# A two-layer decoder on one NeuronCore: the stretch from the routed experts to the third attention put into one table of steps per engine

## What is computed

```
x = x + L0_ffn(layernorm(x))                       # 8 experts of 256, top 2 per token, plus a shared expert
x = x + L1_attn(layernorm(x))                      # per batch and head, 24 of the 128 queries
x = x + L1_xattn(ctx, ctx, layernorm(x), mask)     # all queries against the context

# L1_attn, cut:
q, k, v = proj(Wq, bq), proj(Wk, bk), proj(Wv, bv)
q_norm = jnp.sum(jnp.abs(q), axis=-1)
_, index = jax.lax.top_k(q_norm, u)                # u = 24
scores = where(causal, q @ k.T * scale, -inf)
sel_attn = softmax(take_along_axis(scores, index))
attn_output[index] = sel_attn @ v                  # the other rows stay 0
out = attn_output @ Wo + bo
```

## Time and profile before

| | |
|---|---|
| median of 3 runs | 722.93 us (719.76 to 728.8) |
| the profiled execution | 720.38 us |
| its span, first to last instruction | 718.7 us |
| mean granted clock of TensorE | 0.903 |
| PE busy / DVE / ACT / POOL in the span | 79% / 60% / 40% / 34% |

### The profile page before, as it was taken

One profiled execution on the slowest core, in us unless ns is written; L12 is line 12 of the kernel. 1 busy time (PEld: TensorE's weight loads), 2 busy tenths in 40 slices (PEclk: granted clock), 3 DMA queues, 4 the chain that ended last, 5 costly groups with the idle time before them and its releaser, 6 DMA issues.

```text
span 718.7 us, 14894 instructions
## 1 busy us (share of the span) xinstructions
PE 569.8 (79%) x4679; PEld 413.6 (58%) x4679; DVE 434.5 (60%) x1157; ACT 290.9 (40%) x679; POOL 243.0 (34%) x364
## 2 busy tenths in 40 slices
PE   3689996889987979898727898876989984574992
PEld 1344444566764659897515686643666652454991
DVE  4879887666766575456373465554556624677443
ACT  2675422245555215454203466530435542302660
POOL 6745503301011666253640113224000002372652
PEclk9899999999999979999868899995999988577997
DMA  9974988653500166532301000363445300013114
GB/s 282 326 126 132 277 237 230 162 132 82 135 8 5 42 244 215 170 86 67 79 26 36 0 2 1 100 155 83 126 99 122 70 2 2 0 46 102 34 35 136
DMA packets 87494, 75.72 MB, mean 105 GB/s; under 512 B 10457, under 2 KB 80753, under 8 KB 84513
## 3 DMA queue, kind: packets, MB, share of 16 engines
q1 hardware_dynamic: 82544, 66.80, 34.5%
q0 software_dynamic: 3296, 6.79, 3.2%
q10 hardware_dynamic: 1584, 1.26, 0.6%
HBM read 41.59 MB, written 32.98 MB: 104 GB/s over the span
## 4 chain that ended last, share of the span: by engine, by line
PE 48%; DVE 20%; DMA 9%; issue 8%; POOL 6%; ACT 4%; SPq 3%; DVEq 1%; POOLq 0%; ACTq 0%
PE ps L2330 5%; PE ps L1864 5%; PE ps L2197 3%; PE ps L2162 3%; PE ps L2432 3%; PE ps L2444 3%; PE ps L2342 2%; PE ps L2181 2%; POOL xs_scr L839 2%; PE ps L2158 2%; DMA f<-k_scr 2%; SPq L433 2%; PE ps L2015 2%; PE ps L1860 2%; PE ps L2176 2%
## 5 line engine op out<-in xcount | busy, mean ns | idle before, releaser
L1445 DVE TENSOR_REDUCE negm<-ps 128x4 f32<-128x512 f32 x128 | 84.3, 688 | 57.1 <-PE ps L2162 53.9
L1026 ACT ACTIVATE wa<-ps 128x1024 f32<-128x1024 f32 x64 | 65.5, 1024 | 70.6 <-PE ps L2181 64.5
L2330 PE MATMUL ps<-nT,f 128*128 128x128 f32 x368 | 52.0, 288 | 2.6 <-DVE wb L1657 1.2
L2330 PEld LDWEIGHTS ps<-nT,f 128*128 128x128 f32 x368 | 47.9, 204 | 3.6 <-DVE wb L1657 1.6
L2197 PE MATMUL ps<-wa,f 128*32 128x128 f32 x1024 | 40.2, 284 | 4.0 <-ACT wa L1026 1.5
L1936 PE MATMUL ps<-identb 128*128 128x512 bf16 x100 | 34.2, 401 | 7.8 <-DVE negm L1445 3.9
L710 POOL DMA_INDIRECT x_scr<-y_tok,selT x32 | 31.9, 996 | 23.8 <-ACT stack L1134 10.7
L844 POOL DMA_INDIRECT y_scr<-f,stack x23 | 25.6, 1114 | 30.3 <-DVE f L1803 24.8
L2162 PE MATMUL ps<-stack 75*128 75x128 bf16 x352 | 35.6, 225 | 0.0
L2162 PEld LDWEIGHTS ps<-stack 75*128 75x128 bf16 x352 | 28.4, 101 | 12.2 <-issue 2.4
L1529 DVE COPY f<-w_gu 128x512 f32 x46 | 20.4, 442 | 22.0 <-issue 10.5
(11 more groups left out here) (399 smaller groups left out, 1464.8 us busy)
## 6 DMA issues: line engine op xcount, KB each, us to landing
k_scr<-parts SPq DMA_DIRECT2D x48, 192.0 KB, 3.0
q_scr<-parts SPq DMA_DIRECT2D x48, 192.0 KB, 2.8
stack<-k_scr SPq DMA_DIRECT2D x11, 600.0 KB, 7.2
stack<-q_scr SPq DMA_DIRECT2D x11, 600.0 KB, 5.5
w_w<-in_w SPq DMA_DIRECT2D x2, 2048.0 KB
wb<-q_scr SPq DMA_DIRECT2D x5, 600.0 KB
f<-k_scr SPq DMA_DIRECT2D x5, 600.0 KB
x_scr<-sel SPq DMA_DIRECT2D x2, 1472.0 KB, 10.2
```

The source lines that it names most:

```text
L1026: link.release(act.activation(wa[:, u % 2, :], BF[u % 2], ACT.Exp, scale=SCALE), hWA.filled, hWA.at(stage, n * 4 + u), hB.freed)
L1445: v.tensor_reduce(negm[:, g4 * 4:g4 * 4 + 4, j], A[u % 2].rearrange("p (h k) -> p h k", h=4), AX.X, ALU.max, negate=True).then_inc(hA.free ...
L2330: last = mm(A[x % 2][:, c * S:(c + 1) * S], gu_of[x % NGU][:, c * S:(c + 1) * S], nT[:, k % 2, q * S:(q + 1) * S], start=True, stop=True)
```

## The change

The steps of the five named parts, from tile 21 on, get names of their own, and one table `LATE` per engine gives their order up to the end of the third attention: `tg`, `tk`, `td` are a tile's gate and up product, the turning of a group and the down product, `tc` and `tp` VectorE's weight copy and product, `ts`, `to`, `tn` ScalarE's share; `ga` are the two gathers of one batch; `comb` and `stat` the combine and statistics of a block; `normx` its normalisation, now on ScalarE with scale and bias (GpSimd's `mrstd` makes the two numbers); `turnx`, `projq`, `projk`, `projv`, `tokq`, `heads`, `pick`, `turns`, `seld` the projected pair; `pk`, `pf`, `qp`, `oq`, `pt`, `sc`, `lo`, `ex`, `tu`, `ec`, `sv`, `rc`, `ob`, `pu`, `pl`, `at` the sixteen picked rows; `outp`, `back`, `res`, `stat2`, `rstd2`, `norm2`, `turn2`, `projq2`, `split2` a late block; `A`, `B`, `V`, `M`, `X`, `o`, `x`, `P`, `E`, `N`, `e`, `K`, `s`, `c` the attention's steps as in `WOVEN`. The loop over tiles ends at tile 22; loops in the attention and the order `STEP` go. The first pair's picked rows 0 to 7 come before the second pair's heads; the first eight scores of the attention stand among rows 14 and 15. The 28 warming matmuls go. The first pair's steps rotate over three banks, the second pair's and the late blocks 0 to 2 share `Z`, block 3 uses `T`.

Places in SBUF change with it: keys and queries of the projected pairs move from the gate and up weights to the stack (`room`, over the tiles' rows), the rows' buffers from the stack to the gate and up weights, the picks and the new queries to the down weights, row sums get a tensor of their own; waits for the old users are added. SyncE loads step 0's keys after the second pair's heads, and keys of steps 1 and 2 before the second store; step 3's stack is loaded between the two last stores.

```diff
-        k1 = [flat_gu[:, i * 2 * BT:(i + 1) * 2 * BT] for i in range(2)]
-        q1 = [flat_gu[:, (2 + i) * 2 * BT:(3 + i) * 2 * BT] for i in range(2)]
+        k1, q1 = ([room[:, (2 * i + k) * 2 * BT:(2 * i + k + 1) * 2 * BT] for i in range(2)] for k in range(2))
         spent = w["down"][:, :, :, :].rearrange("p e c d -> p (e c d)")
-        new_q, rest_q = [spent[:, s * BT:(s + 1) * BT] for s in range(2)], spent[:, 2 * BT:3 * BT]
-        pick32, q_bd, e_row, e_col, o_bd, put = ([room[:, (2 * k + s) * HU:(2 * k + s + 1) * HU] for s in range(2)]
+        pick32, q_bd, e_row, e_col, o_bd, put = ([flat_gu[:, (2 * k + s) * HU:(2 * k + s + 1) * HU] for s in range(2)]
                                                  for k in range(6))
-        pick16 = [room[:, 12 * HU + s * HU // 2:12 * HU + (s + 1) * HU // 2].bitcast(bf16) for s in range(4)]
+        pick16 = [spent[:, s * HU // 2:(s + 1) * HU // 2].bitcast(bf16) for s in range(4)]
+        new_q, rest_q = [spent[:, 2 * HU + s * BT:2 * HU + (s + 1) * BT] for s in range(2)], spent[:, 2 * HU + 2 * BT:]
+        norm_T = [oT[:, 0, :], oT[:, 1, :], nT[:, 0, :], nT[:, 1, :]]
...
+        small = sb("row_sums", [128, 6 * NC])
...
+        three = (U, Bk[0][:, 0, :], Bk[1][:, 0, :])
+        first_turns, later_turns = ([s for s in LATE["PE"] if s[:-2] in READ_LATE and place(s) == n] for n in range(2))
+
+        def late_bank(step):
+
+            return (lambda: three[first_turns.index(step) % 3], lambda: Z, lambda: T)[place(step)]()
...
+                sp.wait_ge(gu_done, N0)
+                sp.wait_ge(pe_front, after("heads.1"))
                 load_k(a, 0, slot(0))
-                sp.wait_ge(qk1_ready, 3)
-                load_k(a, 2, slot(2))
                 store_pair("qp2", 0, queries, [], range(1))
                 sp.wait_ge(hP[0].freed, hP[0].free("qp2", 1))
+                sp.wait_ge(down_done, N0)
                 load_q(a, 0, slot(0))
+                sp.wait_ge(dve_front, after("comb.3"))
+                sp.wait_ge(slots_stored[1], 16 * PER)
+                load_k(a, 1, slot(1))
+                load_k(a, 2, slot(2))
                 store_pair("qp2", 0, queries, [], range(1, 2))
                 sp.wait_ge(hP[1].freed, hP[1].free("qp2", 1))
-                sp.wait_ge(attnT_done, 2 * B)
+                sp.wait_ge(scored, HB)
+                sp.wait_ge(q_picked, HB)
                 load_q(a, 1, slot(1))
-                load_k(a, 1, slot(1))
+                store_m(a, 0, slot(0))
+                sp.wait_ge(scored, B)
+                sp.wait_ge(q_picked, B)
                 load_q(a, 2, slot(2))
-                store_m(a, 0, slot(0))
+                store_m(a, 1, slot(1))
                 store_pair("qp2", 1, queries, [], range(1))
-                store_m(a, 1, slot(1))
+                load_stack(a, 3, slot(3))
+                store_m(a, 2, slot(2))
...
+            def gathers(b):
+
+                h = b // HB
+                g.wait_ge(slots_stored[h], 16 * PER)
+                if h == 0:
+                    g.wait_ge(slot_out, NT0 + b + 1)
+                for k, dst in enumerate((y_tok, second)):
+                    g.indirect_dma_start(dst[:, b, :], None, x0_scr[h],
+                                         bass.IndirectOffsetOnAxis(ap=pos0_i[:, k * B + b:k * B + b + 1], axis=0))\
+                     .then_inc(rows_back[b // GB], 16)
+
+            def pick_copy(b):
+
+                g.wait_ge(gu_ready, N0)
+                g.wait_ge(pick16_ready, b + 1)
+                if b > 1:
+                    g.wait_ge(q_picked, b - 1)
+                g.tensor_copy(pick32[b % 2], pick16[b % 4]).then_inc(pick32_ready, 1)
...
+                if kind == "normx":
+                    act.wait_ge(pool_front, after("mrstd.%d" % n))
+                    if n < 2:
+                        act.wait_ge(dve_front, after("te.1"))
+                    else:
+                        act.wait_ge(pe_front, after("turnx.%d" % (n - 2)))
+                    for j in range(GB):
+                        tok = n * GB + j
+                        last = act.activation(xn_tm[:, p, j, :], x_tok[:, tok, :], ACT.Identity, scale=rstd[:, tok:tok + 1],
+                                              bias=from_mean[:, tok:tok + 1])
...
+                elif kind == "absq":
+                    act.wait_ge(pe_front, after("projq.%d" % n))
+                    act.wait_ge(pe_front, after("su.3", "ro.3") if n < 2 else after("heads.0"))
+                    last = act.activation(f[:, p, :], late_bank("projq.%d" % n), ACT.Abs, bias=col["bq1"])
...
+                alone = dict(ec=e_columns, pu=scaled_places, ex=row_exps, at=placed_rows, ts=expert_silu, to=expert_out,
+                             tn=group_nT)
+                for s in WOVEN["ACT"] if a == 0 else LATE["ACT"]:
...
+                if kind == "comb":
+                    v.wait_ge(rows_back[n], 16 * GB * TOPK)
+                    for k, src in enumerate((y_tok, second)):
+                        for b in range(n * GB, (n + 1) * GB):
+                            last = v.scalar_tensor_tensor(out=x_tok[:, b, :], in0=src[:, b, :], scalar=wts[:, k, b:b + 1],
+                                                          in1=x_tok[:, b, :], op0=ALU.mult, op1=ALU.add)
+                        link(last, settle=True)
+                    v.sem_inc(dve_front, 1)
...
+            def row_maxima(b):
+                v.wait_ge(scored, b + 1)
+                if b > 1:
+                    v.wait_ge(e_row_ready, b - 1)
+                v.tensor_reduce(low1[b % 2], A[b % 2][:, 0:HU].rearrange("p (c k) -> p c k", c=NC), AX.X, ALU.max,
+                                negate=True).then_inc(low1_ready, 1)
...
+                    turns, depth = (first_turns, 3) if where == 0 else (later_turns, 1)
+                    turn_no = turns.index(this)
+                    if turn_no >= depth:
+                        read = reader(turns[turn_no - depth])
+                        pe.wait_ge(dict(ACT=act_front, DVE=dve_front)[PLACE[read][0]], after(read))
+                    elif where == 0:
+                        pe.wait_ge(dve_front, after("cc.1", "hd.3"))
+                        pe.wait_ge(act_front, after("sl.3"))
+                    else:
+                        pe.wait_ge(slot_out, N0 - 1)
...
-                keep_warm(T, 14)
...
+            def row_scores(b):
+                pe.wait_ge(pick16_ready, b + 1)
+                if b > 1:
+                    pe.wait_ge(e_row_ready, b - 1)
+                else:
+                    pe.wait_ge(prod_done, N0 - 1 + b)
+                pe.wait_ge(q_bd_ready, b + 1)
+                pe.wait_ge(act_front, after("evk.%d" % (b // GB)))
+                for c in range(NC):
+                    mm(A[b % 2][:, c * S:(c + 1) * S], pick16[b % 4][:, c * S:(c + 1) * S], causal[:, :], start=True,
+                       stop=False, skip_group_check=True)
+                    last = mm(A[b % 2][:, c * S:(c + 1) * S], q_bd[b % 2][:, c * S:(c + 1) * S],
+                              k1[b // HB][:, b % HB * S:(b % HB + 1) * S], start=False, stop=True, skip_group_check=True)
+                last.then_inc(scored, 1)
...
+                    if a == 2 and n == 0 and u < 2:
+                        pe.wait_ge(e_row_ready, B - 1 + u)
...
-            for x in range(N0 + 2):
-                if x < N0:
...
+            for x in range(NT0):
+                gate_up(x)
+                k, q = group_of(x)
+                if q == 0:
+                    slots_in(k + 1)
                 if x >= 2:
...
+                    expert_down(x - 2)
...
+    "PE": """
...
+            tg.45 td.44 turnx.1 projq.0 td.45 projk.0 projq.1 projv.0 tokq.0 heads.0 projk.1 projv.1 tokq.1 turns.0
+            pt.0 qp.0 pt.1 sc.0 qp.1 sc.1 tu.0 sv.0 tu.1 pl.0 sv.1 qp.2 pl.1 pt.2 sc.2 qp.3 pt.3 turnx.2 projq.2
+            sc.3 tu.2 qp.4 tokq.2 sv.2 qp.5 tu.3 qp.6 sv.3 turnx.3 pl.2 pl.3 projq.3 pt.4 pt.5 sc.4 sc.5 heads.1
+            qp.7 outp.0 tu.4 back.0 tu.5 sv.4 tokq.3 pl.4 sv.5 pt.6 sc.6 pl.5 turns.1 projk.2 pt.7 sc.7 tu.6 projv.2
+            sv.6 qp.8 turn2.0 pl.6 qp.9 tu.7 pt.8 sc.8 sv.7 qp.10 projq2.0 pl.7 tu.8 qp.11 outp.1 pt.9 sc.9 sv.8
+            projk.3 pl.8 qp.12 tu.9 pt.10 sc.10 back.1 sv.9 qp.13 pl.9 tu.10 projv.3 pt.11 sc.11 sv.10 pl.10 tu.11
+            pt.12 sc.12 turn2.1 sv.11 qp.14 projq2.1 pl.11 tu.12 pt.13 sc.13 outp.2 sv.12 qp.15 tu.13 back.2 sv.13
+            pl.12 pl.13 pt.14 sc.14 pt.15 sc.15 tu.14 A0.0 turn2.2 A1.0 tu.15 A2.0 A3.0 sv.14 A4.0 projq2.2 sv.15
+            pl.14 A5.0 A6.0 pl.15 A7.0 outp.3 A0.1 A1.1 M0.0 A2.1 back.3 A3.1 A4.1 A5.1 A6.1 B0.0 A7.1 B1.0 B2.0
+            A0.2 V0.0 A1.2 M0.1 B3.0 V1.0 A2.2 V2.0 X0.0 V3.0 A3.2 B0.1 o0.0 B1.1 A4.2 A5.2 turn2.3 A6.2 A7.2
+            projq2.3 V0.1 V1.1 M0.2 B2.1 X1.0 B3.1 o1.0 X0.1 V2.1 V3.1 o0.1 A0.3 A1.3 X1.1 A2.3 o1.1 B0.2 A3.3 A4.3
```

(25 more changed lines are left out.)

994 lines of the change are left out of this document (438 added, 556 removed).

## The result

The changed kernel takes 680.94 us in the median of four runs (679.15 to 683.63), against 721.95 for the kernel before beside it: a ratio of 0.942, 95% interval 0.935 to 0.949. That is 5.8% faster. The forecast was 670, its range 648 to 696. The profiled execution has a span of 679.9 us instead of 718.7.

The account below looks back on a forecast made before the run. Weak stages were taken as latency-bound, engines waiting in fixed order for chains of short operations. Stages 298.5, 46.1, 26.8, 78.4, 8.0, 86.0 and 123.2 gave a span of 667.0; forecast 670 us, range 648 to 696.

Parts of the forecast that it names:

- Parts 1 and 2: Tiles 23 to 45 take 3.0 us more, 46.1; then gathers and first picks, with row 2 starting at 371.4 us.
- Part 3: Rows 2 to 15 with second pair, three late blocks and VectorE's lumps: 78.4 us, rows ending at 449.8 instead of 477.5.
- VectorE's two lumps: Block 3's combine and statistics (4.8 us) and second top-24 chain (4.4), ahead of row work: 7.0 us together.
- it leaves little room: From 344 us on, VectorE's load is 76 of 113 us: not the bound, but with little room.
- Part 4: Start of the third attention: 8 us from rows' end to first transposed score, at 457.8 instead of 500.8.
- Part 5: The third attention's eight steps take 86 us instead of 94.7, ending at 543.8.
- Two DMA waits on the chain go: In the eight steps, the f load (7.55 us) and the last maxima's store (3.18) leave the chain: 10.7 us.
- A tighter weave: Rival, chance 0.16: TensorE never waits in the rows, which take 60.6 us instead of 78.4; whole time 653.
- One bank in a chain: Rival, chance 0.09: second pair and three late blocks share one bank, 24 turns, 19.2 us of waits; whole time 679.
- Loads late: Rival, chance 0.05: step 1's queries and step 3's stack queue behind stores; 10 us at the start and 7.55 stay: 689.
- One row in flight: Rival, chance 0.06: picked rows run one by one at about 8.7 us each instead of 3.55; whole time 743, slower.
- under 4.5 us a row with all else beside them: Sign of being right: from row 2 on, rows pass at under 4.5 us each, all other work included.

Follow-up runs that it names:

- the kernel with three banks: The changed kernel with all second-pair steps ahead of the first row, rotating over three banks, keys and values ahead of the picks' turn: 709.35 us, ratio 0.977.

## Why the prediction was right, and which of its steps failed

**The mechanism** held. The chain that the earlier trace rows named was latency with nothing beside it, and putting rows beside gathers and pair took it away: the stretch gave 43.9 us of the 46.0 predicted, 26.1 of them by that step, going by the kernel with three banks. The second pair ahead of the rows loses all of the kernel's gain, and with three banks most of what was lost is still missing.

**Parts 1 and 2, tiles and gathers,** were right to 0.6 us: 46.1 us as predicted, and 26.2 instead of 26.8 from there to row 2, with ten gathers, then row 2. Warming matmuls left out were costed at nothing; putting them back gained nothing.

**Part 3, the rows:** 82.3 us instead of 78.4, from two errors of opposite sign, so that it is as near as this is luck in part. I had counted 67.2 us of TensorE (49.7 + 9.7 + 7.8) and 11.2 of waits (4.2 for late blocks, 7.0 for VectorE's two lumps). TensorE had 76.65 to do and stood 5.6. The lumps were oversized: the waits for VectorE in the list above are 2.5 us (1.4, 0.7 and 0.4), 7.8 us more on VectorE made the rows 0.9 longer, and "it leaves little room" was wrong. The first scores, beside the last rows, had no price at all in the sum, though they are TensorE's work: without them it is busy 2.9 us less in the rows (73.72 in that kernel's window of 80.64). Products of rows 0 and 1 that slip behind row 2's copy are another 1.7 (93 placing and 90 summing matmuls are 15.5 and 15 rows of six, not 14, at 0.67). The other 4.8 of the 9.4 us I can't lay to one cause.

**Part 4, the start:** 6.8 us instead of 8.0. Load and split of the queries were hidden as said: TensorE stood 0.43 us for them.

**Part 5, the steps,** is the step that failed: 91.9 us instead of 86.0. "Two DMA waits on the chain go", 7.55 + 3.18 us, took a transfer's length in the chain for TensorE's loss. The earlier trace rows had it beside: TensorE was busy 86.16 of 94.7 us there, so all its waits together were 8.5, less than the 10.7 that I let go. The real idle time at the f load was 1.61; the new order in the kernel before gave 1.3 us, and those of busy time, while the idle time stayed 8.3. In the changed kernel the order is needed against a new lateness, worth 13 us.

**Outside the change** I took 298.5 us for granted; the front became 4.1 us longer. From 120 to 145 us the granted clock was 0.80 instead of 0.93, and from 190 to 232 it was 0.96 instead of 1.00, in code that no edit touched. What in the new program moves the clock there wasn't found.

**The rivals.** A tighter weave, 60.6 us from there to the rows' end, lay under TensorE's own 76.65. It took the 0.47 us off each row; but those are a wait of the weight loads, and over four rows of the kernel before TensorE's matmuls were busy all the time, so the pitch of 3.55 was their work already:

```profile
408.29:422.50 14.21, 14.21 (x119) 12.21 (x118) 9.50 (x20) 10.36 (x45) 2.03 (x4) 1.00 0.01 2
```

One bank in a chain gave 679, next to the 680.94 measured, but by another cause: its waits in the rows were 3.1 us and not 19.2. It is real only where the chain stands alone. Loads late did not come true as the kernel is made, and did when the load's place was undone. One row in flight: 14 rows took 5.9 us each with all that lies beside them, where my own sum had 5.6 (78.4/14). The 7.2 at which the gain would have gone counts a row alone; with all beside it, it is 9.3 (5.6 + 51.7/14). For the same reason the sign "under 4.5 us a row with all else beside them" did not fit my sum, and it was missed.

**The bounds.** The highs of the parts add up to 708 rather than 706, and the range of 648 to 696 does not hold the bounds of 644 and 706 that it is said to hold. Neither changes the forecast.

## What to carry to other kernels

When a chain of waits has a long transfer in it, look at how long the engine that is nearly full really stood for it, and sum up that engine's idle time in the stage: no more than that can be won from its waits. When latency-bound work is put beside other work, give a price to everything on the engine that becomes full, what is "pulled ahead" too. To learn which engine that is, double one operation on each: what the stage grows by answers it.

## What the runs showed that I had not expected

Less work on TensorE made a stage slower: with 64 products left out the steps took 102.7 us instead of 91.9, at a granted clock of 0.82 instead of 1.00. The same code, at the same place, ran at either level in different kernels (from 148 to 165 us: 234 matmuls at 1.00, 146 at 0.50). So stages that no edit touched moved by several us, more than some of the effects studied here; stage lengths say more of an edit than the total time.

With nothing beside it, the second pair's chain took 33.5 us on TensorE for 9.7 us of work as the prediction priced it, and three banks and another order in it gave back 14.2 us.
